# Running sums of key-value products: one F32 matmul per half, or two F32R matmuls on a high and a low part

## The reference

```
Z = jnp.einsum('bhsp,bhsn->bhspn', V, K)
Z_cum = jnp.cumsum(Z, axis=2)
Y = jnp.einsum('bhtn,bhtpn->bhtp', Q, Z_cum)
Y = Y.transpose(0, 2, 1, 3).reshape(b, t, d)
return Y @ Wo.T + bo
```

## Time and profile before

| | us |
|---|---|
| median of 3 runs | 1338.17 (1330.79 to 1345.17) |
| the profiled execution, its time | 1333.94 |
| span of its profile | 1332.2 |
| the 32 chunks' sums, from the first to the last, in it | 1051.5 to about 1298 |
| mean granted TensorE clock over the span | 0.883 of full |

### The profile page before, as it was taken

One profiled execution on the slowest core, in us unless ns is written; L12 is line 12 of the kernel. 1 busy time (PEld: TensorE's weight loads), 2 busy tenths in 40 slices (PEclk: granted clock), 3 DMA queues, 4 the chain that ended last, 5 costly groups with the idle time before them and its releaser, 6 DMA issues.

```text
span 1332.2 us, 17322 instructions
## 1 busy us (share of the span) xinstructions
PE 1118.3 (84%) x4988; PEld 812.7 (61%) x4988; DVE 889.5 (67%) x2544; ACT 698.5 (52%) x1314; POOL 619.1 (46%) x725
## 2 busy tenths in 40 slices
PE   5866999991898999999958578999962779999996
PEld 4745877881565777667726466888841445555553
DVE  7746788773687887877727348777753477776561
ACT  4324767771456766667623125777732435445532
POOL 5865000004698888876626752000026556564440
PEclk9658999996899999999975668999985689888897
DMA  7536466751000000000000115577721000000000
GB/s 234 189 137 231 165 227 219 241 181 46 24 15 15 13 16 12 13 5 1 1 0 28 44 39 190 172 240 241 247 91 33 20 16 16 21 24 12 9 11 21
DMA packets 48958, 115.43 MB, mean 87 GB/s; under 512 B 8160, under 2 KB 14304, under 8 KB 48864
## 3 DMA queue, kind: packets, MB, share of 16 engines
q1 hardware_dynamic: 40672, 97.53, 22.4%
q0 software_dynamic: 8192, 16.79, 4.2%
HBM read 79.16 MB, written 35.13 MB: 86 GB/s over the span
## 4 chain that ended last, share of the span: by engine, by line
PE 57%; POOL 14%; DVE 10%; issue 9%; ACT 6%; another core or an unknown queue 3%; DMA 1%; SPq 0%; POOLq 0%; DVEq 0%; ACTq 0%
PE bank L188 6%; PE bank L331 4%; PE bank L332 4%; PE bank L333 4%; PE bank L343 4%; PE bank L345 4%; PE bank L344 4%; PE bank L1384 3%; PE bank L890 2%; PE bank L896 2%; POOL wr L488 2%; PE bank L1405 2%; PE bank L930 2%; PE bank L936 2%
## 5 line engine op out<-in xcount | busy, mean ns | idle before, releaser
L609 DVE TENSOR_TENSOR hid_lo<-hid,hid_hi 128x512 fp32r<-128x512 f32 x248 | 170.2, 688 | 105.4 <-ACT hid L411 92.3
L458 POOL DMA_INDIRECT xs<-spare_all,slots x128 | 132.3, 1034 | 63.0 <-issue 37.4
L488 POOL DMA_INDIRECT got<-ys,y_slots x64 | 67.6, 1057 | 197.4 <-DMA ys<-spare_all 183.4
L411 ACT ACTIVATE hid<-bank,b_up_of 128x512 f32<-128x512 f32 x184 | 125.5, 682 | 6.2
L188 PEld LDWEIGHTS bank<-ident,spare_all 128*128 128x128 f32 x568 | 76.4, 154 | 79.9 <-issue 71.4
L410 ACT ACTIVATE hid_hi<-bank,b_up_of 128x512 fp32r<-128x512 f32 x138 | 95.0, 689 | 45.0 <-PE bank L333 34.2
L188 PE MATMUL bank<-ident,spare_all 128*128 128x128 f32 x568 | 93.2, 295 | 29.4 <-DVE X L624 13.4
L984 ACT ACTIVATE gate_b<-bank,head_rstd 128x128 f32<-128x128 f32 x256 | 72.9, 369 | 55.8 <-POOL head_rstd L1101 55.4
L410 ACT ACTIVATE hid_hi<-bank,cols_sb 128x512 fp32r<-128x512 f32 x48 | 33.0, 688 | 114.0 <-PE bank L333 70.3
L1555 POOL MEMSET wz<- 128x128 f32 x1 | 0.2, 205 | 175.3 <-DVEq L678 175.3
L1647 DVE TENSOR_TENSOR gate_b<-bank,spare_all 128x512 f32<-128x512 f32 x64 | 43.1, 686 | 57.5 <-PE bank L1405 55.6
(11 more groups left out here) (284 smaller groups left out, 3104.3 us busy)
## 6 DMA issues: line engine op xcount, KB each, us to landing
wr<-wq SPq DMA_DIRECT2D x92, 512.0 KB, 4.5
spare_all<-xs SPq DMA_DIRECT2D x46, 256.0 KB, 4.8
ys<-spare_all SPq DMA_DIRECT2D x46, 256.0 KB, 5.0
wq<-wr SPq DMA_DIRECT2D x16, 512.0 KB
got<-in_w_mlp SPq DMA_DIRECT2D x9, 512.0 KB
xs<-X SPq DMA_DIRECT2D x16, 256.0 KB
xs<-spare_all,slots POOLq DMA_INDIRECT x128
out_x<-X SPq DMA_DIRECT2D x8, 256.0 KB, 2.3
```

Source lines behind the costliest of these rows:

```text
L411: nc.scalar.activation(hid[:, n % HC], bank[n % 3][:], ACT.Gelu_apprx_tanh, bias=bias).then_inc(s["gelu_done"], 1)
L458: g.indirect_dma_start(out=xs, out_offset=bass.IndirectOffsetOnAxis(ap=slots[:, k, n:n + 1], axis=0), in_=xn_all[:, n], in_offset=None).th ...
L488: nc.gpsimd.indirect_dma_start(out=rows_of(i, ring)[:, k, b], out_offset=None, in_=ys, in_offset=bass.IndirectOffsetOnAxis(ap=y_slots[:, k ...
L609: v.tensor_tensor(hid_lo[:, q], hid[:, n % HC], hid_hi[:, q].bitcast(F32), ALU.subtract).then_inc(s["lo_done"], 1)
```

## The change

Each half of a chunk's products is now split in two F32R parts, and PE takes the sum of the two in two F32R matmuls that accumulate into one bank. ACT makes the high part (a copy to F32R, `keep_high`), DVE the low part (products minus the high part, `keep_low`). Both parts live in `ws`, once each (not doubled as `kv` is). The triangle is copied to F32R into `before_r` by DVE at the start of the stage.

`keep_high` stands last in ACT's beat. It waits for POOL's products and for PE's sum of the previous chunk. `keep_low` stands on DVE just ahead of `moe_combine`; it waits for `keep_high` and for the same sum. PE's `sums` now wait for `keep_low`, POOL's `products` for `keep_low` of two chunks before.

```diff
+        kv_hi, kv_lo = ([ws[:, h, k] for h in range(2)] for k in range(2))
...
             def sums(g):
                 for h in range(2):
-                    pe.wait_ge(s["kv_ready"], 2 * g + h + 1)
+                    pe.wait_ge(s["kv_lo"], 2 * g + h + 1)
                     if g > 0:
                         pe.wait_ge(s["z_used"], 2 * (g - 1) + h + 1)
-                    nc.tensor.matmul(bank[h][:], tri, kv[g % 2][:, h], start=True, stop=True).then_inc(s["z_in"], 1)
+                    nc.tensor.matmul(bank[h][:], before_r[:], kv_hi[h], start=True, stop=False)
+                    nc.tensor.matmul(bank[h][:], before_r[:], kv_lo[h], start=False, stop=True).then_inc(s["z_in"], 1)
...
-            pe.wait_ge(s["consts"], 2)
+            pe.wait_ge(s["tri_ready"], 1)
...
+            def keep_high(c):
+                for h in range(2):
+                    act.wait_ge(s["kv_ready"], 2 * c + h + 1)
+                    if c > 0:
+                        act.wait_ge(s["z_in"], 2 * (c - 1) + h + 1)
+                    nc.scalar.copy(kv_hi[h], kv[c % 2][:, h]).then_inc(s["kv_hi"], 1)
...
                     keep_projection(here(VK), V)
                     keep_projection(here(VK), K)
+                if chunk_at(beat + 1) is not None:
+                    keep_high(chunk_at(beat + 1))
...
                     if c >= 2:
-                        pool.wait_ge(s["z_in"], 2 * (c - 2) + h + 1)
+                        pool.wait_ge(s["kv_lo"], 2 * (c - 2) + h + 1)
...
+            def keep_low(c):
+                for h in range(2):
+                    dve.wait_ge(s["kv_hi"], 2 * c + h + 1)
+                    if c > 0:
+                        dve.wait_ge(s["z_in"], 2 * (c - 1) + h + 1)
+                    v.tensor_tensor(kv_lo[h], kv[c % 2][:, h], kv_hi[h].bitcast(F32), ALU.subtract).then_inc(s["kv_lo"], 1)
...
             dve.wait_ge(s["consts"], 2)
+            v.tensor_copy(before_r[:], tri).then_inc(s["tri_ready"], 1)
...
                     rest_of_x(here(TURN_3), 2)
+                if chunk_at(beat + 1) is not None:
+                    keep_low(chunk_at(beat + 1))
                 if here(ADD_ROWS) is not None:
                     moe_combine(dve, steps, moe, here(ADD_ROWS), FETCHED_WIDE)
```

More of the change, by code:

```diff
@@ L1320, in l1_sems @@
             return s | {k: sem(f"la_{k}") for k in (
-                "consts", "rows_ready", "xT_ready", "proj_in", "proj_out", "kv_ready", "z_in", "z_used", "y_ready", "s_in", "s_out",
+                "consts", "rows_ready", "xT_ready", "proj_in", "proj_out", "kv_ready", "kv_hi", "kv_lo", "tri_ready", "z_in", "z_used", "y_ready", "s_in", "s_out",
                 "y_in", "yT_out", "o_in", "lo_done", "la_done")}
```

## The result

The changed kernel takes 1445.78 us (median of 6 runs, 1438.14 to 1449.14), the kernel before 1334.48 in the same comparison. The ratio is 1.082 (95% interval 1.078 to 1.086): 8% slower. The forecast was 1430 in a range of 1378 to 1475.

What follows compares the result with a forecast made beforehand. PE was taken to bound the last stage, running nearly without a gap. Gaps of 70 us (20 + 12 + 28 + 14 - 4) and 25 us of lower clock on 1333.94 gave 1429, forecast as 1430, range 1378 to 1475.

Steps and rivals of the forecast that it cites:

- The mechanism: At all four beat ends PE waits for splits standing last in their engines' beats; gaps together 70 us.
- The b0 to b1 term: Before the b1 sums, DVE's beat with the queued combine becomes the chain: 9.6 us instead of 5.43, 28 us in all.
- The b1 to b2 term: Before the b2 sums, copy, cast and subtraction end at 10.2 us instead of 8.39: 1.8 more, 8 times, 14 us.
- the upper bound: 1475 us: the clock also falls in the b1 beat (+36), and subtractions meet POOL at other places (+8).
- The clock term: Clock stays at half from V and K until DOWN_1: 3.5 us more, 7 times, 25 us.
- the rival of a clock low through most of the stage: PE's work outside UP_1 and V/K all at half clock: 1510 us; chance 0.23 for 1455 and more.
- The b3 wait: Before the b3 sums, K's copy, cast, subtractions held by POOL, sums: 2.9 us more, 7 times, 20 us.
- The hold by POOL: At the b3 sums, DVE's subtraction is held over both of POOL's products; 7 subtractions over 2 us long.
- PE's saving: F32R sums take 1.1 us instead of 1.7 to 1.88: 0.6 to 0.7 us a chunk, 20 us over 32.
- the low clock through the b1 beat too: Half clock also in the b1 beat: 1465 us, within the rival of 1455 and more, chance 0.23.
- The faster: Splits hidden before PE reaches its sums, only PE's saving counts: 1310 us, if waits stay under 0.6 us; chance 0.02.
- the unchanged case: Gaps and PE's saving cancel, because half of the beat ends have slack; chance 0.03.

Runs made afterwards that it cites:

- Experiments 5: Changed kernel with only the b3 chunk's cast moved earlier on ACT, ahead of the copies of V and K; 1.051 times the kernel before.
- 6: Changed kernel with only the b0 chunk's cast moved earlier on ACT, ahead of the copies of Q; 1.052 times the kernel before.
- experiment 7: Changed kernel with all four splits placed early in their beats, same instructions; 1.0048 times the kernel before.
- experiment 2: Changed kernel with DVE's moe_combine put ahead of keep_low; 1.075 times the kernel before.
- experiment 3: Changed kernel with six extra matmuls on PE ahead of its wait for the low part, their result overwritten; 1.060 times the kernel before.
- experiment 9: Kernel of 8 with F32 sums on the unsplit products, the parts made but not used; 1.009 times the kernel before.
- experiment 1: Changed kernel with its waits and splits, but F32 sums on the unsplit products; 1.079 times the kernel before.
- 8: Kernel of experiment 7 with POOL's b1, b2, b3 products one beat sooner and b2's cast and low part earlier; 1.016 times the kernel before.
- 11: Kernel of 8 with DVE's low part of b1 moved behind both statistics; 1.023 times the kernel before.

## Why the prediction was right, and where not

**The mechanism was right.** Before, PE hardly waited for the sums' inputs; now the splits stand last in their beats, and the four waits are there, released by the subtraction: 2.4, 2.0, 3.1 and 3.8 us in the period shown. Experiments 5, 6 and 7 take most of them away by order (89 us become 26 in 7), and the time with them.

**That the sum came out near is partly luck.** Of the span, 104 us were measured and 95 forecast, but the terms missed by +5, +11, -4, +3 and -5 us, and these cancel in part.

**The b0 to b1 term was right to 0.1 us per interval** (9.54 against 9.6), and experiment 2 shows the combine's part in it. Without a combine the two intervals were 7.07 and 6.63 against my 6.9. In sum it was 33 instead of 28, because I took 5.43 us as the interval before in every period, and in the first two it had been 2.37 and 3.38.

**The b1 to b2 term was too small:** 14 forecast, 25 measured. I had 10.2 us for each interval, and from the third period on they were 12.0 to 15.0. The missing piece is the half clock in the b1 beat, which I had only in the upper bound (5 us a period) because PE "idles over 5 us" there was what I thought it took. PE idled 5.6 us or more only in the first two periods (6.35 and 5.59) and 3.07 in the one shown, and the clock fell all the same. In the first two periods the term was negative (8.99 and 9.71 against 11.9 and 12.1 before): the long wait for the normalizations, 5.60 us in the earlier trace rows, had moved into the wait for the b1 sums.

**The clock term had about the right size at the wrong place.** I expected half clock from V and K to DOWN_1. It rose at about 1136.9, ahead of Q and DOWN_1, but fell again within the b0 sums (at about 1143.6), and in the b1 beat. The stage was at half for 190 us instead of 49, 54% of it. That is nearer to the rival of a clock low through most of the stage than to my forecast, though the time stayed under the 1465 and 1510 us priced there. As a share of the loss, experiment 3 gives about 30 us, against 25 in my sum.

**The b3 wait:** copy, cast and subtraction were right. The hold by POOL was smaller than the 1.6 us I took from the earlier trace rows: the pair of subtractions took 2.6 us instead of 1.3, and none at this place took over 2 us, where I expected seven. In the changed kernel, POOL and DVE in the same place:

```profile
1131.07 1.07 POOL L1594 TENSOR_TENSOR wa_sb<-spare_all 128x512 f32<-128x512 f32 x1 [4.45 <-ACT spare_all L1515]
1131.54 1.14 DVE L1670 TENSOR_TENSOR ws<-wb_sb,ws 128x512 fp32r<-128x512 f32 x1 [4.59 <-ACT ws L1528]
...
1132.10 1.52 POOL L1594 TENSOR_TENSOR wa_sb<-spare_all 128x512 f32<-128x512 f32 x1
...
1132.61 1.55 DVE L1670 TENSOR_TENSOR ws<-wb_sb,ws 128x512 fp32r<-128x512 f32 x1
```

DVE got in after POOL's first product, and POOL's second took 1.52 us instead of 1.07. That is the rule of the Trainium skill (SBUF — State Buffer, "Who interferes with whom"), which I had weighed and set aside: the two exclude each other for one instruction, whoever comes first. Here the trace agrees. But the earlier trace rows isn't wrong either, and at 1165.01 a subtraction in the changed kernel took 2.38 us across both of POOL's products, having started 0.28 us after the first began. What decides between the two isn't settled.

**PE's saving was the term that failed.** I priced it at 0.6 to 0.7 us a chunk, 20 us in all, from rows at full clock (1.1 us for four, at 0.28) and took it as given in every term. Even at full clock the four rows took about 1.3 us (in experiment 7 from 1085.62 to PE's next work at 1086.88), with 0.34 us between the rows of a pair that had waited, and at half clock they were as long as F32 rows at full clock. In PE's busy time the F32R sums saved 6.4 us in experiment 9 and cost 6.7 in experiment 1, and in the time neither shows any gain.

The rival that came nearest besides is the low clock through the b1 beat too (1465 against 1446 measured). The faster and the unchanged case failed on the condition named: at no beat end was the wait under 0.6 us, the shortest being 1.7. Of the other signs, the periods (44 to 51 us in the first six, 42 to 47 forecast) and the stage (352 us, 340 forecast) came out somewhat longer.

## What stays open

Why the kernel with all splits early doesn't beat the one before. PE (204 of 253 us busy), DVE (211) and the chain through POOL's roots and ACT's normalizations may each be too long there, which isn't shown; moving one wait (8, 11) brought another. How much of the gain in 5 and 6 is the clock, and why the clock stays higher with F32 sums at the same waits (0.84 against 0.72), is open too. No kernel tried was faster than the one before.

## To carry to other kernels

Where an engine that bounds a stage starts each round with a certain step, a new link in front of that step can cost its own latency plus everything that stands ahead of it in its engine's program, however idle that engine is on average. Look for the earliest place in each engine's order at which the input exists: here that place was worth 101 of 108 us, with the same instructions. And price a saving of TensorE work at the clock that the new rhythm leaves: with gaps of mostly 2 to 4 us per beat and the shorter sums between them the clock was at half in over half of the stage, and nothing of the saving was left in the time.

## What the runs showed of the hardware

- Idle gaps of 2 us ahead of the b0 sums were followed by half clock (0.50 from 1143.6 to 1146.8), not only gaps of over 5 us as in the earlier trace rows.
- Matmuls that compute nothing of use made a kernel 2% faster (1.060 against 1.083), with the mean granted clock of the stage at 0.90 instead of 0.72.
- With the same waits, the stage had a mean granted clock of 0.84 with F32 sums and 0.72 with the shorter F32R sums.
- An F32R row of a sum took as long at half clock (0.43 us from start to start) as an F32 row at full clock.
- POOL's products slow down as well when they meet DVE's subtraction: 1.52 us instead of 1.07.
